# Scores of the first attention in four 32-row tiles: half-heads in blocks of partitions instead of masked keys

## Chip, core and metric

One Trainium2 chip (trn2), one of its cores. The metric is device time in microseconds of the whole launch. Each figure is the median of several runs; one further execution is profiled.

## What is computed

Four batch rows of 512 tokens with 128 features pass through four blocks, each followed by a residual addition and a layer norm: a differential attention, a feed-forward net with weights and activations quantised to 4 bits, a causal attention with rotary positions (16 query heads, 4 key heads), and a mixture of 8 experts. The change touches the first attention alone:

```python
q, k, v = to_heads(q), to_heads(k), to_heads(v)       # 16 heads of 8
q1, q2 = jnp.split(q, 2, axis=-1)                      # half-heads of 4
k1, k2 = jnp.split(k, 2, axis=-1)
a1 = softmax(einsum('bhsd,bhtd->bhst', q1, k1) * scale)
a2 = softmax(einsum('bhsd,bhtd->bhst', q2, k2) * scale)
out = einsum('bhst,bhtd->bhsd', a1 - lam * a2, v)      # then RMS norm, output projection
```

So there are 32 half-heads, each with 512 x 512 scores over a contraction of only 4 numbers. The scores are computed in bf16, with each number split in three bf16 parts and six products of parts kept (`NTERM = 6`), so a half-head's scores take 6 x 4 = 24 rows of contraction.

## The kernel before

**Rows of the batch.** Each engine runs `body` once for each of the four batch rows (first, a loop of two, last). At the end of a row every engine adds to `row_ended`, SP clears semaphores and opens the next row (`open_row`, L352 its increments). A row holds, in order: the first attention (the loop over `s` from -4 to 17), the end of the previous row's mixture of experts together with this row's first output projection and feed-forward net, and then the second attention, which ends with the projection at L1384. While the second attention runs, the next batch row's first-attention projection is computed, split by POOL into parts (`split_next`) and reordered through DRAM by SP (`store_parts`, `load_terms`).

**Operands of the scores.** 8 groups `g` of 4 half-heads `j`. `qst` and `kst` hold all four half-heads of a group on 96 partitions (6 terms x 16). To pick out one half-head, DVE writes `kpad[:, g, j]`, which is `kst` times a mask that zeroes the 72 rows of the other three (`keys_of_next`, 32 tensor_scalars a row, L546; 24 of them at s == 3 of the second attention and 8 at s == 4). Every scores matmul contracts over all 128 partitions.

**Two passes.** For each half-head and tile of 128 queries, PE first computes scores (L1185, 128 matmuls a row), of which DVE takes the negated maximum along the keys (L726, `mx`). Group by group POOL splits the 128 x 16 maxima into three bf16 parts (`max_parts`), PE transposes them (L1192), DVE copies them out as `mrow` (L732), and SP moves them by DMA into rows 96 to 107 of `qst` (L358). The second pass (L1177, 128 matmuls) computes the transposed scores, with the maxima subtracted by those extra rows; ACT takes the exponential (L981). The values product (L1210) follows: for each quarter-tile four matmuls write to four blocks of 32 output partitions; ACT copies the result out (L972), PE transposes it (L1199), DVE keeps it (L737).

**The order around it.** PE's instructions are in one hand-written order. At each step (s, c), c from 0 to 3: two scores matmuls of the second pass (banks 0 to 2 in rotation, each waiting for the exponential three before), two of the first pass, 13 steps ahead (banks 3 to 5 in rotation, each waiting for the maximum three before), and in steps c = 1 and 2 one values product of four matmuls. Group g's second pass starts at s = 2g, c = 0 and waits there for its maxima to have landed (`max0_in`); its transposition L1192 and copy L732 stand at s = 2g - 1, c = 1. So one group takes two s, that is eight steps: 16 matmuls and 16 maxima of the first pass, 16 matmuls and 16 exponentials of the second, four values products. The first-pass maxima end at s = 12.

**Row data and SP.** In a row SP issues one DMA at each of the eight groups and waits for it. In the second attention it issues two for each of its four groups (L366); after the second group it issues 2 stores (L323) and 12 loads (L331) for the next row. POOL clears the unused rows 96 to 127 of `kst` and `qst` with three memsets after the third group (`clear_terms`, L451 to L454), while DVE, in rows 1 to 3, runs the scaling of the mixture's layer norm (L640) at s == 1.

## Time and profile before

| | |
|---|---|
| median of 3 runs | 1578.21 us (1576.48 to 1590.58) |
| the profiled execution | 1577.19 us, its span 1575.4 us |
| PE busy | 1289.6 us, 82% of the span |
| DVE busy | 851.7 us, 54% |
| ACT busy | 666.1 us, 42% |
| POOL busy | 107.2 us, 7% |
| mean granted TensorE clock | 0.891 |
| first attention, rows 0 to 3, about | 60 to 180, 396 to 518, 764 to 886, 1134 to 1256 us |

The span is the time from the first to the last instruction; 1.8 us of the profiled execution lie outside it. Busy shares are means over stages with different limits; the stages have to be read one by one.

### The profile page before, as it was taken

The page shows a single profiled execution, that of the slowest core. Times are in us where ns is not written, and L with a number is a line of the kernel's source. Part 1 is how long each engine was busy: PE and PEld are TensorE (multiplying, and loading weights), DVE is VectorE, ACT ScalarE, POOL GpSimd, SP SyncE. Part 2 cuts the span into 40 slices and gives each one's busy share as a digit, 9 for nine tenths or more (in the row PEclk, how much of TensorE's full clock was granted, in tenths as well). Part 3 has the DMA queues.
Part 4 walks back from the last instruction along what each step waited for, and adds up shares of the span by engine and source line. Part 5 has one row for each costly group of instructions (what it writes and reads, how often), then busy time and mean ns, then how long its engine had stood idle before and what let it go on. Part 6 is the DMA issues. An engine that isn't in the chain of part 4 may idle for free.

```text
span 1575.4 us, 19401 instructions
## 1 busy us (share of the span) xinstructions
PE 1289.6 (82%) x7257; PEld 643.8 (41%) x7257; DVE 851.7 (54%) x1816; ACT 666.1 (42%) x1407; POOL 107.2 (7%) x250
## 2 busy tenths in 40 slices
PE   2499458788898998788799899878789899878888
PEld 1122133445122564344322365444422267344556
DVE  6587446333785467433677365624578456633222
ACT  1067323352376442343166542254157643235232
POOL 4000001020000000020000000003000000000000
PEclk6599769799799999889699999889989999879989
DMA  7400000030000000030000000030000000000000
GB/s 149 111 2 2 8 0 1 21 41 2 1 2 2 1 7 1 1 61 9 2 2 2 1 7 1 1 61 2 7 1 2 1 1 1 1 1 1 8 1 8
DMA packets 31731, 21.04 MB, mean 13 GB/s; under 512 B 12873, under 2 KB 29329, under 8 KB 31633
## 3 DMA queue, kind: packets, MB, share of 16 engines
q1 hardware_dynamic: 31632, 19.75, 6.3%
q8 instruction: 59, 0.97, 0.3%
q14 instruction: 40, 0.32, 0.1%
HBM read 14.96 MB, written 4.19 MB: 12 GB/s over the span
## 4 chain that ended last, share of the span: by engine, by line
PE 64%; DVE 18%; ACT 7%; SPq 4%; issue 3%; DMA 2%; POOL 0%; DVEq 0%; POOLq 0%; PEldq 0%; ACTq 0%; another core or an unknown queue 0%
PE ps L1210 8%; PE ps L1142 8%; PE ps L1152 7%; DVE mx L726 6%; PE ps L1177 6%; PE ps L1291 6%; PE ps L1312 5%; PE ps L1185 5%; PE ps L1281 4%; ACT ps L1038 3%; PE ps L1324 3%; DVE mx L843 2%; DVE SH L817 2%; PE ps L1384 2%; ACT PROB L981 2%
## 5 line engine op out<-in xcount | busy, mean ns | idle before, releaser
L981 ACT ACTIVATE PROB<-ps 128x512 f32<-128x512 f32 x512 | 272.4, 606 | 284.0 <-PE ps L1177 283.9
L726 DVE TENSOR_REDUCE mx<-ps 128x1 f32<-128x512 f32 x512 | 318.7, 683 | 86.0 <-PE ps L1185 85.9
L1185 PE MATMUL ps<-KPAD,SH 128*128 128x512 bf16 x512 | 193.8, 431 | 54.9 <-SPq L352 35.0
L1038 ACT ACTIVATE ps<-ps,mx 128x128 f32<-128x128 f32 (+3 forms) x256 | 127.1, 497 | 252.6 <-DVE mx L843 252.6
L1312 PE MATMUL ps<-KPAD,SH 64*128 64x384 f32 (+3 forms) x512 | 171.4, 530 | 58.4 <-ACT ps L1038 50.2
L843 DVE TENSOR_REDUCE mx<-ps 128x1 f32<-128x128 f32 (+3 forms) x256 | 113.6, 486 | 189.8 <-PE ps L1315 189.8
L1177 PE MATMUL ps<-SH,KPAD 128*128 128x512 bf16 x512 | 163.3, 395 | 15.2 <-ACT PROB L981 9.9
L1291 PE MATMUL ps<-SH,KPAD 64*128 64x256 f32 (+3 forms) x512 | 139.5, 536 | 40.1 <-DMA m1row<-mrow 22.9
L1210 PE MATMUL ps<-PROB,v 128*32 128x512 f32 x1024 | 138.0, 614 | 6.8 <-ACT SH L972 4.7
L959 ACT ACTIVATE KPAD<-ps,b_sb 128x512 f32<-128x512 f32 x128 | 87.9, 687 | 126.8 <-PE ps L1142 126.4
L1312 PEld LDWEIGHTS ps<-KPAD,SH 64*128 64x128 f32 x512 | 79.9, 219 | 117.7 <-ACT ps L1038 98.2
L1142 PE MATMUL ps<-xnT,w_sb 128*128 128x512 f32 x256 | 126.9, 632 | 0.4
L1152 PEld LDWEIGHTS ps<-w_sb,KPAD 128*128 128x128 f32 x1024 | 118.7, 192 | 13.4 <-issue 13.4
L1185 PEld LDWEIGHTS ps<-KPAD,SH 128*128 128x128 bf16 x512 | 51.5, 101 | 166.2 <-DVE mx L726 91.6
L1152 PE MATMUL ps<-w_sb,KPAD 128*128 128x128 f32 x1024 | 118.9, 275 | 0.0
L1177 PEld LDWEIGHTS ps<-SH,KPAD 128*128 128x128 bf16 x512 | 40.6, 99 | 168.2 <-ACT PROB L981 143.7
L1056 ACT ACTIVATE PROB<-ps 128x1024 f32<-128x1024 f32 x80 | 81.2, 1020 | 44.4 <-PE ps L1296 44.4
L1324 PE MATMUL ps<-PROB,KPAD 128*64 128x256 f32 (+3 forms) x512 | 77.4, 444 | 12.2 <-DVE SH L832 12.2
L817 DVE SCALAR_TENSOR_TENSOR SH<-ps,bqk,rope_sb 128x512 f32<-128x512 f32 x96 | 67.5, 745 | 34.1 <-PE ps L1281 33.7
L1291 PEld LDWEIGHTS ps<-SH,KPAD 64*128 64x128 f32 x512 | 63.9, 214 | 48.9 <-DMA m1row<-mrow 25.6
L697 DVE SCALAR_TENSOR_TENSOR KPAD<-ps,rt,KPAD 128x128 f32<-128x128 f32 x112 | 31.5, 344 | 72.7 <-PE ps L1152 72.0
L1142 PEld LDWEIGHTS ps<-xnT,w_sb 128*128 128x128 f32 x256 | 43.2, 198 | 66.3 <-ACT KPAD L959 47.1
(175 smaller groups left out, 1361.9 us busy)
## 6 DMA issues: line engine op xcount, KB each, us to landing
SH<-qk_parts SPq DMA_DIRECT2D x48, 128.0 KB, 6.4
qk_parts<-SH SPq DMA_DIRECT2D x8, 384.0 KB, 2.9
w_sb<-in_L_ffn_W_dram SPq DMA_DIRECT2D x1, 2048.0 KB
XN<-in_L_attn_x_dram SPq DMA_DIRECT2D x4, 256.0 KB, 2.9
out_dram<-XP SPq DMA_DIRECT2D x4, 256.0 KB, 2.3
wq_sb<-in_L_attn_Wq_dram SPq DMA_DIRECT2D x1, 512.0 KB, 5.4
rope_sb<-in_rope_dram SPq DMA_DIRECT2D x1, 512.0 KB
wo_sb<-in_L_attn_Wo_dram SPq DMA_DIRECT2D x1, 512.0 KB
```

Source lines behind the costliest of these rows:

```text
L726: dve.tensor_reduce(mx[:, ga % 2, r % 16:r % 16 + 1], ps[:, 3 + r % 3, :], AX, ALU.max, negate=True).then_inc(max0_done, 1)
L843: dve.tensor_reduce(mx[:, ga % 2, col:col + 1], ps[:, A1_BANK[r % 3], 0:w], AX, ALU.max, negate=True).then_inc(max1_done, 1)
L981: act.activation(prob0[:, n % 2, c, k], ps[:, q % 3, :], ACT.Exp, scale=float(HD0) ** -0.5).then_inc(exp0_done, 1)
L1038: act.activation(tile, tile, ACT.Exp, bias=mx[:, (s + 1) % 2, col:col + 1], accum_out=lsum[:, (s + 1) % 2, 0, col:col + 1]).then_inc(sum1_ ...
L1142: pe.matmul(ps[:, f % 2, :], w1_sb[:, e, P * f:P * (f + 1)], xnT[:, :], start=True, stop=True).then_inc(up_ready, 1)
L1152: ins = pe.matmul(ps[:, 2 + d % 2, P * t:P * (t + 1)], hE[:, d % 2, f, P * t:P * (t + 1)], w2_sb[:, d, f, :], start=(f == 0), stop=(f == 3))
L1177: pe.matmul(ps[:, q % 3, :], kpad[:, g, c, P * kt:P * (kt + 1)], qst[:, g, :], start=True, stop=True).then_inc(s0_ready, 1)
L1185: pe.matmul(ps[:, 3 + r % 3, :], qst[:, a // 8, P * qt:P * (qt + 1)], kpad[:, a // 8, j, :], start=True, stop=True).then_inc(a0_ready, 1)
L1210: ins = pe.matmul(ps[32 * j:32 * j + 32, 6, :], v0[:, kt, 2 * (m // 2) + j // 2, :], prob0[:, m % 2, j, c - 1, :], start=(kt == 0), stop=( ...
L1291: pe.matmul(dst[i], k1[half(i), g, lo:lo + P], qT[half(i), 2 * g + pair, lo:], start=True, stop=False)
L1312: pe.matmul(dst[-1], qT[half(r % 2), 2 * g + pair, P * qt:P * (qt + 1)], k1[half(r % 2), g, 0:w], start=True, stop=False)
L1324: ins = pe.matmul(ps[64 * h:64 * h + 64, 6, P * kt:T], v1[:, kt, D1 * s:D1 * (s + 1)], prob1[:, s % 2, 2 * p_ + h, POFF[kt]:POFF[kt] + WID ...
```

## The change

Each half-head of a group gets a block of 32 partitions of its own: block j holds in its rows 0 to 23 the 24 rows of half-head j, and in rows 24 to 26 the three parts of its maxima (`kst` has ones there). A scores matmul contracts over the 27 (second pass) or 24 (first pass) partitions of its block alone. The masked keys `kpad`, their 32 DVE instructions a row and the mask are gone; `clear_terms` is gone, and one memset at the start writes the ones of `kst`. `qst` and `kst` are tensors of their own. Consecutive matmuls go to different blocks (j = q % 4, j = r % 4), and which half-heads form a group has changed, so the maxima's columns, the values' index and the views of the output change with it. The terms are laid out in DRAM by the stores: 12 stores of 128 KB (one for each term of q and k) in place of 2 of 384 KB, and 8 loads of 192 KB in place of 12 of 128 KB. The maxima of a group go to `qst` by three DMAs (one for each part, to four partitions 32 apart), waited for together, instead of one.

```diff
-M_ROW = NTERM * 16
+M_ROW = NTERM * 4
...
-        KPAD = sb("KPAD", [P, NG * HF * T], BF16)
+        KPAD = sb("KPAD", [P, 12288], BF16)
...
-        qst = SH[:, 0:2048].bitcast(BF16).rearrange("p (g n) -> p g n", g=NG)
-        kst = SH[:, 2048:4096].bitcast(BF16).rearrange("p (g n) -> p g n", g=NG)
+        qst = sb("qst", [P, NG, T], BF16)
+        kst = sb("kst", [P, NG, T], BF16)
...
-                for c in range(2):
+                for c, part in enumerate((Q_PART, K_PART)):
                     sp.wait_ge(parts_ready, c + 1)
-                    sp.dma_start(parts_dram[c].rearrange("s p n -> p s n"), split[:, c]).then_inc(parts_out, 16)
-                sp.wait_ge(parts_out, 32)
+                    for t in range(NTERM):
+                        dst = terms_dram[c, t].rearrange("d j g n -> (j g) d n")
+                        sp.dma_start(dst, split[:, c, part[t]]).then_inc(parts_out, 16)
+                sp.wait_ge(parts_out, 16 * 2 * NTERM)
...
-                for c, (dst, part) in enumerate(((kst, K_PART), (qst, Q_PART))):
-                    for t in range(NTERM):
-                        src = parts_dram[1 - c, part[t]].rearrange("(g r) n -> r g n", g=NG)
-                        sp.dma_start(dst[16 * t:16 * t + 16], src).then_inc(terms_in, 16)
+                for c, dst in ((1, kst), (0, qst)):
+                    for j in range(HF):
+                        src = terms_dram[c].rearrange("t d j g n -> j (t d) g n")[j]
+                        sp.dma_start(dst[32 * j:32 * j + M_ROW], src).then_inc(terms_in, 16)
...
                 for g in range(NG):
                     sp.wait_ge(mrow_ready, g + 1)
-                    sp.dma_start(qst[M_ROW:M_ROW + 12, g, :], mrow[:, :]).then_inc(max0_in, 16)
-                    sp.wait_ge(max0_in, 16 * (g + 1))
+                    for s in range(3):
+                        sp.dma_start(qst[M_ROW + s::32, g, :], mrow[16 * s:16 * s + 16, :]).then_inc(max0_in, 16)
+                    sp.wait_ge(max0_in, 48 * (g + 1))
...
             pool.memset(ones3[:, :], 0.0).then_inc(setup_pool, 1)
+            pool.memset(kst[:, :, :], 1.0).then_inc(setup_pool, 1)
...
-                    if not last and g == 2:
-                        pool.wait_ge(mparts_ready, NG + 3)
-                        clear_terms()
...
-                for g in groups:
-                    for j in range(HF):
-                        dve.tensor_scalar(kpad[:, g, j, :], kst[:, g], jmask[:, j:j + 1], None, ALU.mult).then_inc(keys_ready, 1)
...
+                                col = 4 * (r % 4) + r % 16 // 4
...
-                                dve.tensor_reduce(mx[:, ga % 2, r % 16:r % 16 + 1], ps[:, 3 + r % 3, :], AX, ALU.max,
+                                dve.tensor_reduce(mx[:, ga % 2, col:col + 1], ps[:, 3 + r % 3, :], AX, ALU.max,
...
-                    if not last and s in KEYS_AFTER:
-                        keys_of_next(KEYS_AFTER[s])
...
-                                pe.matmul(ps[:, q % 3, :], kpad[:, g, c, P * kt:P * (kt + 1)], qst[:, g, :],
+                                pe.matmul(ps[:, q % 3, :], kst[rows, g, P * kt:P * (kt + 1)], qst[rows, g, :],
...
-                                pe.matmul(ps[:, 3 + r % 3, :], qst[:, a // 8, P * qt:P * (qt + 1)], kpad[:, a // 8, j, :],
+                                pe.matmul(ps[:, 3 + r % 3, :], qst[rows, a // 8, P * qt:P * (qt + 1)], kst[rows, a // 8, :],
...
-                                ins = pe.matmul(ps[32 * j:32 * j + 32, 6, :], v0[:, kt, 2 * (m // 2) + j // 2, :],
+                                ins = pe.matmul(ps[32 * j:32 * j + 32, 6, :], v0[:, kt, 4 * j + m // 4, :],
```

## Rows read from the trace of the kernel before

**Rows 1.** Stretches of the timeline: us, PE (x) PEld DVE ACT POOL busy, PEclk, DMA, GB/s.

```profile
396.00:409.00 13.00, 11.84 (x21) 2.19 (x21) 12.96 (x27) 0.00 (x0) 0.83 (x4) 0.55 0.00 0
...
447.00:459.70 12.70, 12.43 (x70) 3.76 (x70) 10.42 (x20) 9.00 (x18) 0.83 (x4) 1.00 0.01 3
```

**Rows 2.** The chain that ended last, row 1's first attention: start, us on it, what.

```profile
447.52 0.17 PE ps L1192
447.69 0.99 PE ps L1210 x8
448.69 0.54 PE ps L1177 x2
...
460.08 0.17 PE ps L1192
```

**Rows 3.** Timeline of the same period, DVE: start, us, line, operation, operands.

```profile
445.19 3.68 DVE L726 TENSOR_REDUCE mx<-ps 128x1 f32<-128x512 f32 x6 [0.68 <-PE ps L1185]
...
448.79 0.21 DVE L732 COPY mrow<-ps 48x128 bf16<-48x128 bf16 x1
```

**Rows 4.** Timeline, the hop of one DMA from maxima to second pass, row 1.

```profile
408.56 0.85 SPq L358 DMA_DIRECT2D SH<-mrow  x1
...
410.62 1.03 PE L1177 MATMUL ps<-SH,KPAD 128*128 128x512 bf16 x2 [0.82 <-DMA SH<-mrow]
```

**Rows 5.** Timeline, a hop of two DMAs in row 0's second attention.

```profile
308.77 1.45 SPq L366 DMA_DIRECT2D m1row<-mrow  x2
...
311.47 1.72 PE L1291 MATMUL ps<-SH,KPAD 64*128 64x512 f32 x4 [3.04 <-DMA m1row<-mrow]
```

**Rows 6.** Timeline of PE, a pair in two 64-row tiles and its successor.

```profile
644.06 0.64 PE L1296 MATMUL ps<-m1row,ones 64*128 64x512 bf16 x2
644.49 0.64 PE L1312 MATMUL ps<-KPAD,SH 64*128 64x128 f32 x4
```

**Rows 7.** A stretch of row 1's second attention, columns as in rows 1.

```profile
608.00:612.00 4.00, 2.37 (x18) 1.51 (x19) 2.85 (x8) 0.87 (x5) 0.00 (x0) 1.00 0.00 0
```

**Rows 8.** Timeline, the transpositions of groups 1 and 7 in row 1.

```profile
420.95 0.24 PE L1192 MATMUL ps<-identb,mparts 128*48 128x128 bf16 x1
...
498.17 0.24 PE L1192 MATMUL ps<-identb,mparts 128*48 128x128 bf16 x1
```

**Rows 9.** The chain at the ends of row 0 and row 3.

```profile
368.07 2.33 PE ps L1324 x16
371.03 6.38 DVE KPAD L546 x24
...
384.57 7.43 PE ps L1384 x64
...
1470.80 2.30 PE ps L1324 x16
...
1485.57 7.43 PE ps L1384 x64
```

**Rows 10.** The chain up to group 2's hop in rows 1 and 3, second attention.

```profile
687.39 2.33 PE ps L1324 x16
690.82 4.14 DVE XP L640 x3
695.77 1.91 DMA m1row<-mrow
...
1431.93 2.31 PE ps L1324 x16
1438.35 1.89 DMA m1row<-mrow
```

**Rows 11.** Timeline of SP's queue, second attention of row 0.

```profile
315.14 5.53 SPq L331 DMA_DIRECT2D SH<-qk_parts  x12
334.87 27.94 SPq L366 DMA_DIRECT2D m1row<-mrow  x4
```

**Rows 12.** Timeline of SP's queue at the start of the program.

```profile
22.40 5.53 SPq L331 DMA_DIRECT2D SH<-qk_parts  x12
```

More of the change, by code:

```diff
@@ L335, in give_out @@
                 sp.dma_start(out_rows[bass.ds(row, 1)].rearrange("a p t e -> (a p) t e"), XP[:, :, :]).then_inc(row_out, 16)
-            late = [terms_in, kst_edge, keys_ready, mparts_ready, mrow_ready, max1_in, s1_ready, exp1_done, av1_done,
+            late = [terms_in, mparts_ready, mrow_ready, max1_in, s1_ready, exp1_done, av1_done,
                     oT_ready, y_ready, ln_done, row_out, dve_order, pool_order]
@@ L377, in body @@
                 if not last:
-                    sp.wait_ge(terms_in, 16 * 2 * NTERM)
+                    sp.wait_ge(terms_in, 16 * 2 * HF)
                 open_row()
@@ L412, in _ @@
             pool.memset(ones3[:, :], 0.0).then_inc(setup_pool, 1)
+            pool.memset(kst[:, :, :], 1.0).then_inc(setup_pool, 1)
             pool.memset(eps[:, 0:1], LN_EPS).then_inc(setup_pool, 1)
             pool.memset(eps[:, 1:2], RMS_EPS).then_inc(setup_pool, 1)
-            pool.wait_ge(setup_pool, 6)
+            pool.wait_ge(setup_pool, 7)
             pool.memset(v0[:, :, :, HD0:HD0 + 1], 1.0).then_inc(setup_pool, 1)
             for half in range(2):
-                pool.wait_ge(setup_pool, 7 + half)
+                pool.wait_ge(setup_pool, 8 + half)
                 pool.memset(ones3[64 * half:64 * half + 3, :], 1.0).then_inc(setup_pool, 1)
-            pool.wait_ge(setup_pool, 9)
+            pool.wait_ge(setup_pool, 10)
             def next_row(done, n):
@@ L445, in split_next @@
                     pool.tensor_tensor(split[:, c, 2], rem[:, c], split[:, c, 1], ALU.subtract).then_inc(parts_ready, 1)
-            def clear_terms():
-                pool.wait_ge(parts_ready, 2)
-                pool.wait_ge(parts_out, 32)
-                step(pool.memset(kst[96:128], 0.0))
-                settle()
-                pool.memset(kst[M_ROW:M_ROW + 12], 1.0).then_inc(kst_edge, 1)
-                step(pool.memset(qst[96:128], 0.0))
-                settle()
-                pool.wait_ge(kst_edge, 1)
             def body(first, last):
@@ L496, in body @@
                         split_next((1,))
-                    if not last and g == 2:
-                        pool.wait_ge(mparts_ready, NG + 3)
-                        clear_terms()
                 next_row(mparts_ready, NG + NKV)
             split_next((0, 1))
-            clear_terms()
-            next_row(kst_edge, 1)
+            next_row(parts_ready, 2)
             body(True, False)
@@ L614, in _ @@
             setup(dve.tensor_scalar(bqk[:, 1], bqk[:, 1], rot_sign, None, ALU.mult))
-            keys_of_next(range(NG))
             settle_setup()
@@ L758, in body @@
                     experts_input()
-                step(dve.tensor_scalar(rs[:, :, 1::2], rs[:, :, 1::2], lam[:, 0:1], None, ALU.mult)); settle()
+                rs_u = SH2[:, 1152:1280].rearrange("p (a u x) -> p u a x", a=4, u=2)
+                o_u = SH2[:, 0:1152].rearrange("p (a u x d) -> p u a x d", a=4, u=2, d=HD0 + 1)
+                step(dve.tensor_scalar(rs_u[:, 1], rs_u[:, 1], lam[:, 0:1], None, ALU.mult)); settle()
                 for u in range(2):
-                    w = rs[:, :, u::2].rearrange("p g (h a) -> p g h a", a=1).broadcast_to([P, NG * NT, 2, HD0])
-                    step(dve.tensor_tensor(od[:, u], oall[:, :, u::2, 0:HD0], w, ALU.mult))
+                    w = rs_u[:, u].rearrange("p a (x b) -> p a x b", b=1).broadcast_to([P, 4, 4 * NT, HD0])
+                    step(dve.tensor_tensor(od[:, u], o_u[:, u, :, :, 0:HD0], w, ALU.mult))
                 settle()
@@ L889, in body @@
                         step(dve.tensor_tensor(X[:, :, :], X[:, :, :], bow, ALU.add))
-                    if not last and s in KEYS_AFTER:
-                        keys_of_next(KEYS_AFTER[s])
                 dve.wait_ge(oT_ready, 2 * NKV)
                 settle()
-                if last:
-                    next_row(oT_ready, 2 * NKV)
-                else:
-                    next_row(keys_ready, HF * NG)
-            next_row(keys_ready, HF * NG)
+                next_row(oT_ready, 2 * NKV)
+            next_row(v0_ready, 1)
             body(True, False)
@@ L980, in body @@
                             act.wait_ge(s0_ready, q + 1)
-                            act.activation(prob0[:, n % 2, c, k], ps[:, q % 3, :], ACT.Exp,
+                            act.activation(prob0[:, n % 2, q % 4, q % 8 // 4], ps[:, q % 3, :], ACT.Exp,
                                            scale=float(HD0) ** -0.5).then_inc(exp0_done, 1)
```

46 lines of the change are left out of this document (21 added, 25 removed).

## Prediction

> **What bounds the kernel now.** I read the page first, for the busy shares. PE leads with 82%, but the shares are means over unlike stages, so I next asked for the busy times of the first attention alone. In its steady part PE is busy 12.43 of 12.70 us, DVE 10.42, ACT 9.00, at the full clock (1.00, that is 2.4 GHz) [rows 1]. The chain that ended last shows the same: it stays on PE from one transposition L1192 to the next, 460.08 - 447.52 = 12.56 us for one group of four half-heads [rows 2]. In that period lie four values products of 0.99 us (4.0), transpositions (0.6 with those of the output) and sixteen pairs of scores matmuls, which take the other 7.8: 0.49 a pair, one right after a values product 0.54 [rows 2]. 512 columns at 2.4 GHz are 0.213 us, so the matmuls of a pair run one after the other. So PE is the bound here, and its scores are more than half of it.
>
> What comes next if they get cheaper is DVE: six maxima back to back take 3.68 us, 0.613 each [rows 3], so sixteen of them and the copies cannot go under 10.4 [rows 1]. The most that the change can give in this loop is therefore about 2.1 us a period, six periods a row, four rows: 50 us of 1575. The lead-in before it is on DVE already: 12.96 of 13.00 us [rows 1], and gains nothing.
>
> **The scores matmuls.** Two matmuls in different 64-row tiles already run at once in this kernel: a bf16 pair over 512 columns starts at 644.06 and its successor at 644.49, 0.43 us later, at the half clock, where 512 columns of a single one are 0.427 [rows 6]. Four tiles of 32 rows are not in the trace. I bound a step's four matmuls (now two pairs, 0.97 us) by 0.22 (all at once) and 0.97 (none), and take 0.3, since each step's four lie in four different blocks and banks but wait for different engines. The Trainium skill (TensorE: Matmul & The Clock Gate, Part 3) gives 3.07 times for four row tiles; by it the estimate is 0.28, which would change nothing below. PE's work in a period then falls from 12.4 to 4.0 + 8 x 0.3 + 0.6 = 7.0 us, and PE waits instead of working.
>
> **The hop of the maxima.** Each group's second pass waits for the maxima to go round: DVE copy, SP, DMA, PE. One DMA takes 2.06 us from SP's issue to the matmul (410.62 - 408.56) [rows 4]. Two cost 2.70 (311.47 - 308.77), since an issue holds SP for 0.72 [rows 5]. The change makes three. Their issue price is not in the trace; they have fewer pieces each, so I bound it by 0.46, the price of the large loads [rows 11], and by 0.85, the single one here [rows 4]. That gives 2 x 0.50 + 1.96 = 2.9 to 2 x 0.85 + 1.96 = 3.7 us; I take 3.4, from the pair, which is the nearest row.
>
> This hop was hidden in PE's order and now it is not. After DVE's copy of group g+1 (0.2 us, estimated from the like copies) PE has only two steps left before it stands at the second pass of g+1. Behind that wait in PE's order stand the first pass's matmuls, so DVE runs dry as well: it has four maxima left (2.45 us) against 3.4. From PE's release to the next copy DVE must then take twelve maxima. So the period has a chain of its own: 0.2 + 3.4 + 0.5 (first matmul to DVE) + 12 x 0.613 = 11.5 us. This, and not DVE's 10.4, is the new floor, 1.1 under the 12.56. ACT (9.0) stays below.
>
> **The clock.** PE will be busy 7.0 of 11.5 us and stand still for about 1.8 us in one piece at the hop (3.4 less the two steps). Now it is busy nearly all the time at 1.00 [rows 1]. The rows pull both ways: 2.37 busy of 4.00 us goes with 1.00 in the second attention [rows 7], while the lead-in, PE busy 11.84 of 13.00 with single matmuls paced by DVE, has 0.55, the half clock [rows 1]. I expect one fall to the half clock (1.2 GHz) in most periods. What it costs: the values product of 0.99 us becomes 2.0, once or twice, of which DVE's three banks (1.84 us of maxima) hide the larger part. I take 0.8 us a period, with 0 and 2 as bounds. Period: 12.3.
>
> **The first attention, summed.** In row 1 the stretch from group 1's transposition to group 7's is 498.17 - 420.95 = 77.2 us [rows 8], six periods of 12.56 and 1.8 us of extras (a norm on DVE, a slow first period). With 12.3 it is 73.8, and the norm, now on the chain, leaves about 0.4: 74.2, so 3 us saved, in each of rows 1 to 3. In row 0 there are no extras and the longer hop shows once at group 0 (1.4): 1 us. At group 0 of the other rows DVE's wait grows likewise, but there ACT's table loads hold PE later anyway. After the maxima end, pairs of second-pass scores and values products alternate with ACT; 0.8 us less a row, 3 in all. Sum: 9 + 1 + 3 = 13 us. Bounds: a period of 11.3 (short hop, full clock) gives 24 more; 14 gives 41 less.
>
> **The masked keys.** 24 of DVE's 32 instructions lie at s == 3 and take 6.38 us, 0.27 each [rows 9]. They are on the chain: the copy of the next values product waits behind them, and PE behind that. Row 3 prepares no next row and is what remains without them: from the same values product to L1384 it takes 1485.57 - 1470.80 = 14.77 us, row 0 takes 384.57 - 368.07 = 16.50 [rows 9]. So 6.4 us of work is worth 1.7, three times: 5 us. The other eight lie beside the 7.43 us of L1384 and are free either way.
>
> **The memsets of POOL.** In rows 1 and 2 DVE's scaling of the norm, four short instructions, runs beside `clear_terms` and three of them hold the chain for 4.14 us; it stands ahead of the copy that feeds the next hop [rows 10]. The way from the values product to the hop is 695.77 - 687.39 = 8.38 us there and 1438.35 - 1431.93 = 6.42 in row 3, which has no memsets [rows 10]. So 2.0 us twice: 4. Where the memsets stay without a norm (row 0), nothing.
>
> **The transfers.** In a row 12 stores replace 2 and 8 loads 12: six more issues of 0.46 us [rows 11] and twice the stored bytes, behind the second hop. SP's next duty comes at 334.87, and the old loads end at 320.7 [rows 11], so 14 us of cover; even 8 us more of waiting and issuing stays inside. Were it gone, the third hop would be late by the difference. At the start of the program there is no cover: SP's queue is the chain there until the first row opens, and the old loads begin at 22.40 [rows 12]. Ten more stores add 4.6 us, four fewer loads give 1.8 back, and the doubled bytes land later, 1 or 2 us: 4 us lost, bounds 2.8 and 8. The new 128-partition memset of POOL there lies before anything that it delays.
>
> **Sum.** 13 + 5 + 4 - 4 = 18 us off the profiled execution's 1577.2 (span 1575.4 and 1.8 around it): 1559. The median before, 1578.2, is 1 us above that execution.
>
> **Rivals.** (a) The clock holds, or the three issues are cheap. For it: rows 7, where PE is busy 59% at 1.00. Against: the standstill at the hop is longer than any in the loop now. Period 11.3 to 11.7, so 24 periods shorter by 0.8 in the middle: 1559 - 19 = 1540, far end 1535. Chance 0.22. (b) The clock is at half for a large share of the loop. The Trainium skill (TensorE: Matmul & The Clock Gate, Part 1) says that throttled is the default and that activity releases it; here that would mean that relieving PE slows it. As a mechanism of this kernel: the values products then cost 2.0 each and the scores 0.5 a step, 8 + 4 + 1.2 = 13.2 us of PE work, and with the standstill of 1.8 the period is 15.0 if always cold and about 13.4 if half the time. At 13.4 the loop loses 1.1 x 24 = 26 against my 12.3: 1585, inside 1%. It decides against the change from a period of about 13.7 on (1593), and always cold gives 1559 + 65 = 1624. For it: the lead-in's 0.55. Against: a cold PE is busy nearly all of its time, and in this trace it came back to 1.00 when it was. Chance of slower by over 1%: 0.15. (c) The 32-row matmuls do not overlap, so that the change doesn't do what it says: then a period is PE's 12.4 and the standstill, about 13.9, or 1597. Against: the pair of rows 6. Chance 0.05. (d) Hop and clock together just eat the gain, period 12.8 to 13.5: 1571 to 1588. Chance 0.18. My forecast, a period of 12.0 to 12.8: 1552 to 1571, has 0.40.
>
> **How the numbers follow.** 1% is 16 us, about what a measurement of this kernel tells from no change. Faster by over 1% is under 1562: all of (a) and some 0.35 of the forecast's cases: 0.57. Within 1%: the rest of the forecast, (d), and a little of (c): 0.25. Slower: 0.18. The range reaches from near (a)'s far end, 1537, to 1592, which leaves (b)'s cold cases and part of (c) outside. The likeliest case's own range is 1552 to 1571.
>
> **What would show it.** In the profile after: transpositions L1192 12.3 us apart (now 12.56), PE busy about 60% in the loop, SP's three issues and the matmul 3.4 us after the first, DVE idle about 1 us in a group with the DMA as releaser; a granted clock in the loop that alternates; the first maximum of row 0 some 4 us later than 60; a second attention that ends like row 3's in every row. The prediction is wrong if the period is near 10.4 (the hop is covered), or over 13 (the clock), or if the start of the program costs more than 8 us.

## The result, and the profile after

| | before | after |
|---|---|---|
| median of 20 runs each | 1581.78 us (1575.84 to 1590.58) | 1590.17 us (1583.35 to 1601.45) |
| the profiled execution | 1577.19 us, span 1575.4 | 1594.19 us, span 1592.4 |
| PE busy | 1289.6 us, 82% | 1281.6 us, 80% |
| DVE busy | 851.7 us, 54% | 805.3 us, 51% |
| mean granted TensorE clock | 0.891 | 0.826 |

The ratio of the two is 1.0049, 95% interval 1.0029 to 1.0069: half a per cent slower, where 1.1% faster was forecast. Medians here and below are over all runs, while ratios leave out those more than 1.5% above the fastest of the same kernel. The two profiled executions differ by twice the difference of the medians, 17 us. In the changed kernel the second pass is L1153 (was L1177), the first pass L1162 (L1185), the maxima L703 (L726), the transposition of the maxima L1169 (L1192), the values product L1187 (L1210), the hop's DMAs L357 (L358), and the first matmul of the mixture of experts, which follows the attention in rows 1 to 3, L1116 (L1142); in row 0 the output projection follows, L1204 (L1227).

From the page of the changed kernel: busy time of each engine, the granted clock in 40 slices, and the groups of the attention's matmuls (busy us, mean ns | idle before, what ended most of it).

```profile
PE 1281.6 (80%) x7257; PEld 618.5 (39%) x7257; DVE 805.3 (51%) x1688; ACT 664.8 (42%) x1407; POOL 68.0 (4%) x239
PEclk6578769799587899799678599889868699879989
...
L1162 PE MATMUL ps<-kst,qst 24*128 24x512 bf16 x512 | 177.7, 483 | 56.3 <-SPq L350 37.9
...
L1187 PE MATMUL ps<-PROB,v 128*32 128x512 f32 x1024 | 192.4, 837 | 7.4 <-ACT SH L946 4.1
L1153 PE MATMUL ps<-qst,kst 27*128 27x512 bf16 x512 | 155.4, 466 | 46.5 <-ACT PROB L955 30.3
```

The same from the page of the kernel before:

```profile
PEclk6599769799799999889699999889989999879989
...
L1210 PE MATMUL ps<-PROB,v 128*32 128x512 f32 x1024 | 138.0, 614 | 6.8 <-ACT SH L972 4.7
```

A matmul of the values product, whose shape and number the change leaves alone, takes 837 ns on the mean instead of 614, 54 us more busy time in all. The clock slices say why: where the first attentions lie, most slices of 7 to 9 come down by one to four tenths.

Stretches of the third batch row (called row 2, the first being row 0): first from the transposition of group 0 to that of group 7 (the loop), then from there to about the end of the attention (the tail). Columns as in [rows 1]. Kernel before, then after:

```profile
775.00:866.00 91.00, 85.05 (x438) 25.10 (x437) 70.32 (x126) 60.40 (x114) 5.79 (x28) 0.94 0.01 2
866.00:891.00 25.00, 18.85 (x115) 6.58 (x115) 7.67 (x31) 15.20 (x29) 0.00 (x0) 0.95 0.01 1
```

```profile
784.00:875.00 91.00, 77.52 (x440) 17.91 (x439) 71.33 (x127) 60.52 (x115) 5.80 (x28) 0.76 0.01 2
875.00:908.00 33.00, 26.92 (x113) 7.84 (x112) 7.24 (x30) 14.68 (x28) 0.00 (x0) 0.55 0.00 1
```

The loop is as long as before, with 7.5 us less work on PE but a clock of 0.76. The tail has the same order of instructions and takes 8.9 us longer (33.51 against 24.62), at 0.55. Its chain after, in row 2 (start, us on it, what), shows PE's own matmuls with ACT between them; each values product has 1.9 us on it, against 0.99 in [rows 2]:

```profile
886.21 1.86 PE ps L1187 x8
888.07 0.54 PE ps L1153 x2
888.61 1.87 PE ps L1187 x8
890.48 0.58 PE ps L1153 x3
...
891.54 0.82 ACT PROB L955 x2
...
903.09 0.59 ACT SH L946
```

The whole difference of the profiled executions, summed over the four rows from the first instructions of each line (the second attention is taken up to the first matmul of its output projection):

| stretch | before | after | change | forecast |
|---|---|---|---|---|
| start of the program to the first maximum | 60.1 | 63.2 | +3.1 | +4 |
| loop, groups 0 to 7 | 359.0 | 356.5 | -2.4 | -10 |
| tail, group 7 to the first matmul after the attention | 102.0 | 127.5 | +25.5 | -3 |
| from there to the end of the second attention | 880.8 | 871.7 | -9.1 | -9 |

These make +17.1, against 17.0 between the spans; what the table leaves out is 173.5 us in both. The tails are 28.13, 24.62, 24.62 and 24.62 us before and 30.44, 30.06, 33.51 and 33.51 after.

### The profile page after: what moved, and what is told of

Its sections match the earlier page's. It is cut to its first block, busy times and chain, and to the rows that moved or that the text cites. A ratio compares the mean times of both kernels' runs of the same rounds, so it can differ in the third digit from the quotient of the medians.

```text
span 1592.4 us, 19325 instructions
## 1 busy us (share of the span) xinstructions
PE 1281.6 (80%) x7257; PEld 618.5 (39%) x7257; DVE 805.3 (51%) x1688; ACT 664.8 (42%) x1407; POOL 68.0 (4%) x239
## 4 chain that ended last, share of the span: by engine, by line
PE 62%; DVE 17%; ACT 9%; SPq 5%; issue 4%; DMA 3%; POOL 0%; DVEq 0%; POOLq 0%; PEldq 0%; ACTq 0%; another core or an unknown queue 0%
PE ps L1187 11%; PE ps L1116 8%; PE ps L1126 7%; PE ps L1268 7%; DVE mx L703 6%; PE ps L1289 5%; PE ps L1153 5%; PE ps L1258 4%; PE ps L1301 4%; ACT PROB L955 3%; ACT ps L1012 3%; DVE mx L822 2%; DVE SH L796 2%; PE ps L1361 2%; SPq L392 2%
## 5 line engine op out<-in xcount | busy, mean ns | idle before, releaser
L703 DVE TENSOR_REDUCE mx<-ps 128x1 f32<-128x512 f32 x512 | 318.6, 683 | 102.9 <-PE ps L1162 101.3
L1162 PE MATMUL ps<-kst,qst 24*128 24x512 bf16 x512 | 177.7, 483 | 56.3 <-SPq L350 37.9
L1289 PE MATMUL ps<-KPAD,SH 64*128 64x512 f32 (+3 forms) x512 | 173.6, 537 | 58.7 <-ACT ps L1012 50.5
L1187 PE MATMUL ps<-PROB,v 128*32 128x512 f32 x1024 | 192.4, 837 | 7.4 <-ACT SH L946 4.1
L1153 PE MATMUL ps<-qst,kst 27*128 27x512 bf16 x512 | 155.4, 466 | 46.5 <-ACT PROB L955 30.3
L1153 PEld LDWEIGHTS ps<-qst,kst 27*128 27x128 bf16 x512 | 33.2, 94 | 261.6 <-ACT PROB L955 200.4
L1116 PE MATMUL ps<-xnT,w_sb 128*128 128x512 f32 x256 | 127.4, 634 | 0.4
L1162 PEld LDWEIGHTS ps<-kst,qst 24*128 24x128 bf16 x512 | 37.9, 94 | 120.5 <-DVE mx L703 73.6
L796 DVE SCALAR_TENSOR_TENSOR SH<-ps,bqk,rope_sb 128x512 f32<-128x512 f32 x96 | 67.5, 745 | 31.7 <-PE ps L1258 31.4
L1116 PEld LDWEIGHTS ps<-xnT,w_sb 128*128 128x128 f32 x256 | 43.4, 199 | 66.7 <-ACT KPAD L933 47.2
```

Of the source, the lines that this page charges most:

```text
L703: dve.tensor_reduce(mx[:, ga % 2, col:col + 1], ps[:, 3 + r % 3, :], AX, ALU.max, negate=True).then_inc(max0_done, 1)
L1116: pe.matmul(ps[:, f % 2, :], w1_sb[:, e, P * f:P * (f + 1)], xnT[:, :], start=True, stop=True).then_inc(up_ready, 1)
L1153: pe.matmul(ps[:, q % 3, :], kst[rows, g, P * kt:P * (kt + 1)], qst[rows, g, :], start=True, stop=True).then_inc(s0_ready, 1)
L1162: pe.matmul(ps[:, 3 + r % 3, :], qst[rows, a // 8, P * qt:P * (qt + 1)], kst[rows, a // 8, :], start=True, stop=True).then_inc(a0_ready, 1)
L1187: ins = pe.matmul(ps[32 * j:32 * j + 32, 6, :], v0[:, kt, 4 * j + m // 4, :], prob0[:, m % 2, j, c - 1, :], start=(kt == 0), stop=(kt == 3))
L1289: pe.matmul(dst[-1], qT[half(r % 2), 2 * g + pair, P * qt:P * (qt + 1)], k1[half(r % 2), g, 0:w], start=True, stop=False)
```

## The experiments

Times are medians, ratios those to the kernel before in the same series, with their 95% intervals. The median of the kernel before lies between 1578.77 and 1583.98 us in these series, so kernels of different series are better compared by their ratios. Of each edit the main lines are shown. "Tail" and "loop" are the stretches above; where four numbers stand, they are rows 0 to 3.

**Fill the tail.** The changed kernel with one matmul over the full array added to each step of the tail, into a bank that nobody reads.

```diff
+                        if 13 <= s <= 16:
+                            if s == 13 and c == 0:
+                                pe.wait_ge(max0_done, 16 * NG)
+                            pe.matmul(ps[:, 3, :], kst[:, 0, 0:P], kst[:, 1, :], start=True, stop=True)
```

> The changed kernel, with one more matmul (128 partitions, 512 columns, into the unused bank 3, read by nobody) in each of the 16 steps of s = 13 to 16, after the first attention's maxima have ended. Theory (clock): the loss sits after group 7's transposition, where PE, relieved of half of its scores time, stays at the half clock (0.55 and 0.69 there in the changed kernel, 0.95 before) and the values products cost 1.93 us in place of 1.00. The added work should bring the clock back: the stretch from group 7's transposition to L1116 falls from 33.5 and 30.0 us to about 25 in rows 1 to 3, and the total by 15 to 22 us to 1568 to 1575, faster than the kernel before. Rival (tiling drains or ACT bound the tail): 16 more matmuls of 0.21 to 0.43 us only add work; the stretch stays at 30 to 35 us and the total is 1590 to 1600.

1588.02 us (10 runs), 1.0042 (1.0007 to 1.0076). Tails 29.02, 28.02, 29.92, 29.93 at a clock of 0.89, 0.87, 0.77, 0.77. So added work over all rows of the array raises the clock of the tail and shortens it by 1.4 to 3.6 us, less than the 5 to 8.5 forecast. The total gains nothing that can be told.

**All four matmuls of a step in one block.** PE gets its old amount of work back, since the tiles no longer overlap, but with 24 and 27 rows.

```diff
-                                j, kt = q % 4, 2 * (n % 2) + q % 8 // 4
+                                j, kt = c, 2 * (n % 2) + k
...
-                                j, qt = r % 4, r % 16 // 4
+                                j, qt = (a + 3) % 4, 2 * (a % 8 // 4) + u
```

> The changed kernel with only the order of half-heads changed: the four scores matmuls of a step lie in the same block of 32 partitions (j = c for the second pass, the same block for the first pass), so they can't overlap. Contraction stays 27 and 24 rows, keys and transfers stay as changed. Clock theory: PE is busy with scores as long as before (0.85 us a step), so the clock comes back to about 0.9 in the first attention and the tail to about 25 us; the loop's period is PE's 12.5 to 13. Total 1565 to 1578, faster than the changed kernel by 12 us or more although its matmuls no longer overlap. Rival 1 (the clock follows the rows in use, 27 of 128): it stays at half for much of the loop, and serial matmuls at half clock give 1610 or more. Rival 2 (the clock is not the cause): without overlap the period rises, total 1595 to 1610.

1816.07 us (4 runs), 1.147 (1.138 to 1.157): 15% slower, with periods of 21.02 us. A stretch of one period in row 1, columns as in [rows 1]:

```profile
541.00:562.00 21.00, 21.00 (x73) 4.48 (x69) 10.46 (x18) 9.06 (x17) 0.81 (x5) 0.50 0.00 1
```

and three successive lines of PE's timeline there:

```profile
526.83 1.03 PE L1153 MATMUL ps<-qst,kst 27*128 27x512 bf16 x2
527.66 1.05 PE L1162 MATMUL ps<-kst,qst 24*128 24x512 bf16 x2
528.64 1.94 PE L1187 MATMUL ps<-PROB,v 128*32 128x512 f32 x8
```

PE is busy in all of the 21.00 us, its scores run one after the other (0.83 us from one pair to the next), and the clock stays at 0.50. I had expected that a busy PE brings the clock back. Here it doesn't: of the 21 us some 13 (sixteen pairs of 0.83) go to matmuls over 24 and 27 rows. The standstill at the hop is not what holds the clock here: there is none.

**The hop alone.** The kernel before, its one DMA of the maxima split in three.

```diff
-                    sp.dma_start(qst[M_ROW:M_ROW + 12, g, :], mrow[:, :]).then_inc(max0_in, 16)
-                    sp.wait_ge(max0_in, 16 * (g + 1))
+                    for s in range(3):
+                        sp.dma_start(qst[M_ROW + 4 * s:M_ROW + 4 * s + 4, g, :], mrow[16 * s:16 * s + 16, :]).then_inc(max0_in, 16)
+                    sp.wait_ge(max0_in, 48 * (g + 1))
```

> The kernel before, with its one DMA for the maxima of a group split into three of 4 partitions each, waited for together, as in the changed kernel: the longer hop alone. The hop should take 2.9 us instead of 2.06 (the changed kernel's issues take 0.52 us each). In PE's full order the slack is about 0.8 us, so if the hop is only a small part of the loss the total is within 5 us of the kernel before (1582 +- 5). Rival (the hop is the loss): the period rises by about 0.9 us, six times four, and the total is 1595 or more.

1594.12 us (10 runs), 1.0084 (1.0043 to 1.0126). Each period grows by 0.2 us, 12.56 to 12.75. In its profile, whose span is 23.6 us longer than that of the kernel before, the loops are 7.8 us longer in all and the tails 2.2; the rest lies outside the first attention. The three DMAs take 0.63 us each to issue here (median; 1.96 to 2.13 for the three). The total lies between the two expectations. So the longer hop has a price even where PE has other work behind it, and it isn't what lengthens the tail by 25 us.

**Fill the loop too.** As the first, and one full-array matmul ahead of each step's first-pass pair.

```diff
+                                if u == 0 and s >= 0:
+                                    pe.matmul(ps[:, 3 + r % 3, :], kst[:, 0, 0:P], kst[:, 1, :], start=True, stop=True)
```

> As the first run, and in addition one matmul of 128 partitions and 512 columns in each step with first-pass scores from s = 0 on, written to the bank of that step's first matmul just ahead of it (which overwrites it). It leaves PE's real work as changed and adds about 1.7 us of it in a period. Clock theory: the clock in the loop rises from 0.74 to 0.88 to nearly 1.00, the period falls from 12.0 to 13.9 to about 11.5 to 12.0, and the total is 1555 to 1568. Rival: the hop's standstill still throws the clock to half, and the added work only costs: no better than the run with the tail filled, 1570 to 1580.

1802.88 us (4 runs, 1802.21 to 2223.92), 1.139 (1.127 to 1.151). The periods are 21.35 us at 0.50. A full-array matmul between the two narrow pairs of a step ends the overlap of the pairs with each other: each of the step's three pieces now follows the one before by 0.54 us, as these lines of PE's timeline show. (The two matmuls of a pair still overlap; in one block a pair took 0.83.) One such matmul a step doesn't bring the clock back in the loop, and the total is far from the forecast 1555 to 1568.

```profile
528.04 0.60 PE L1153 MATMUL ps<-qst,kst 27*128 27x512 bf16 x2
528.58 0.61 PE L1167 MATMUL ps<-kst 128*128 128x512 bf16 x1
529.12 0.60 PE L1168 MATMUL ps<-kst,qst 24*128 24x512 bf16 x2
```

By these lines about 12 of the 21.35 us go to matmuls over 128 rows (eight added ones of 0.54 and four values products of 1.9, an estimate), and the clock is 0.50 all the same.

**The rows alone undone.** The changed kernel, all of its scores contracted over 128 partitions again.

```diff
-                                rows = slice(32 * j, 32 * j + M_ROW + 3)
+                                rows = slice(0, P)
...
-                                rows = slice(32 * j, 32 * j + M_ROW)
+                                rows = slice(0, P)
```

> The changed kernel with one thing undone in the scores matmuls: all of them contract over all 128 partitions instead of 24 or 27. (It leaves out the separation of the half-heads: each scores tile is the sum over the four of its group, and the exponential's scale is 1e-9 so that all stays finite; instructions, sizes, waits and transfers are otherwise the changed kernel's.) The run with all four of a step in one block showed PE fully busy at 0.5 through the loop, so a busy PE alone does not hold the clock. Theory (the clock follows how much of the array the matmuls drive): with full rows the clock in the loop is 0.94 to 0.96 as before, the period about 12.75 as in the kernel before with the three-part hop, the stretch after group 7 about 25 us, and the total 1575 to 1590. Rival (the cold clock comes from something else in the change, the operands' place, their ones, the three-part hop): the clock stays at half and the total is over 1750, as in the one-block run, since the matmuls cannot overlap.

1571.58 us (10 runs), 0.9969 (0.9932 to 1.0005). The same two stretches of row 2:

```profile
777.00:868.00 91.00, 84.36 (x437) 24.67 (x436) 70.29 (x126) 60.16 (x114) 5.83 (x28) 0.94 0.01 2
868.00:894.00 26.00, 19.65 (x115) 6.10 (x114) 7.34 (x30) 15.34 (x30) 0.00 (x0) 0.92 0.01 1
```

The number, order and columns of the operations are those of the changed kernel. Besides the rows three things differ: the exponential is scaled by 1e-9, so that all probabilities are near 1, `qst` is zeroed once, and the matmuls of a step no longer overlap. Clock 0.94 and 0.92 instead of 0.76 and 0.55, periods 12.55, tails 28.10, 25.85, 25.82, 25.78. The overlap isn't the cause of the low clock, since the run in one block has none, keeps PE without a gap, and is at 0.50; nor are the values, since the kernel before computes the real ones over 128 rows at 0.94. The zeroing stands at the start of the program. What is left is the matmul over 24 or 27 rows in a block of 32. Whether it is the number of rows or the addressing of a 32-row block that counts, no run separates.

**The rows in the tail alone, and in the loop alone.** Two kernels that split the run before at s = 13: in the first the tail is over 128 rows and the loop narrow, in the second the reverse (there the first pass is wide too).

```diff
+                                rows = slice(0, P) if s >= 13 else slice(32 * j, 32 * j + M_ROW + 3)
...
+                                rows = slice(0, P) if s < 13 else slice(32 * j, 32 * j + M_ROW + 3)
...
+                                rows = slice(0, P)
```

> The new kernel with the scores matmuls over all 128 partitions from step s = 13 on (the tail, second pass only); the loop keeps its 24 and 27 rows. As in the run with all rows wide, the separation of the half-heads is left out there, the exponential is scaled by 1e-9 and qst is zeroed at the start; neither changes the number or size of the operations. Theory 1 (the narrow contraction of the tail's own matmuls keeps the clock down in the tail): tails of 25 to 27 us at a clock of 0.85 or more in rows 1 to 3 (now 30.1, 33.5, 33.5 at 0.56 to 0.68), loop as now (0.75 to 0.81, periods near 12.5); total 15 to 22 us under the new kernel, ratio to the kernel before 0.992 to 0.996. Theory 2 (the tail inherits the loop's clock, or stays low because PE waits for ACT there): tails stay at 30 to 33.5 us at 0.56 to 0.7; ratio 1.004 to 1.006.

> The complement: scores matmuls over all 128 partitions up to step s = 12 (both passes), and the 27 rows in four blocks from s = 13 on. The same parts are left out as in the run before. Theory 1: the loop is that of the kernel before (periods 12.55, clock 0.94 or more), and then the clock falls inside the tail, although it came in warm: tails of 29 to 33 us at 0.6 to 0.75; ratio to the kernel before 1.000 to 1.006. Theory 2 (the tail inherits the loop's clock): tails of 24.5 to 26 us at 0.9 or more; ratio 0.994 to 0.998. It also shows whether the values in the scores (here nearly constant probabilities) have a part in the clock: if they did, this tail too would be at 0.9.

Tail wide: 1578.86 us (10 runs), 0.9978 (0.995 to 1.0006), tails 29.69, 25.79, 25.76, 25.76. Loop wide: 1586.9 us (10 runs), 1.0028 (0.9995 to 1.0062), tails 28.91, 28.47, 27.15, 26.95. Loop and tail of row 2 in the first:

```profile
784.00:876.00 92.00, 79.17 (x437) 17.87 (x437) 70.52 (x126) 59.99 (x114) 5.83 (x28) 0.76 0.01 2
876.00:902.00 26.00, 19.49 (x114) 6.24 (x114) 7.66 (x31) 15.08 (x29) 0.00 (x0) 0.91 0.00 1
```

and in the second:

```profile
779.00:871.00 92.00, 83.77 (x430) 24.84 (x438) 70.66 (x126) 60.41 (x114) 5.80 (x28) 0.95 0.01 2
871.00:898.00 27.00, 20.47 (x114) 6.05 (x114) 7.21 (x30) 15.14 (x29) 0.00 (x0) 0.79 0.00 1
```

A tail of wide matmuls comes out at 0.91 although the loop ahead of it ran at 0.76. A tail of narrow ones falls to 0.79 although it came in from a loop at 0.95: its values products take 1.11 us at 878.72 and 1.93 at 880.29. So the tail's own matmuls set most of its clock; the probabilities are near 1 in both runs, so their values don't make this difference. The second run's tails, 26.95 to 28.91 us at 0.78 to 0.83, lie between the ranges of the two theories: what the tail inherits from the loop has a part too. But the two don't simply add. Summed over the rows from group 0 to the end of the attention:

| loop / tail | wide | narrow |
|---|---|---|
| wide | 464.0 | 472.6 |
| narrow | 468.3 | 484.1 |

The narrow tail costs 8.7 us behind a warm loop and 15.8 behind a cool one. One cell is not like the others: narrow with narrow is the changed kernel with its real probabilities, the other three have them near 1. With real ones, wide with wide is 461.0 (the kernel before), and the narrow loop is 356.5 us where it is 361.3 with those near 1, so in these two the values matter little; for a narrow tail behind a narrow loop no run shows it. The first of these two kernels was expected 15 to 22 us under the changed one and came out 11 under it in the median (0.7% by the ratios); its attention stretches alone give 15.8, the low end. The profiled execution of the second is the fastest of its ten (1578.17 us), that of the first the slowest (1586.10), so these sums hold for the stretches, not for the totals.

**The kernel before without `clear_terms`.** `kst` gets its own tensor with ones written once, and the contractions stop at row 96 or 108, so that POOL's memsets can go.

```diff
-                    if not last and g == 2:
-                        pool.wait_ge(mparts_ready, NG + 3)
-                        clear_terms()
...
-                                pe.matmul(ps[:, q % 3, :], kpad[:, g, c, P * kt:P * (kt + 1)], qst[:, g, :],
+                                pe.matmul(ps[:, q % 3, :], kpad[0:M_ROW + 12, g, c, P * kt:P * (kt + 1)], qst[0:M_ROW + 12, g, :],
```

> The kernel before with one part of the change alone: the memsets of POOL in each row (clear_terms) taken away. kst gets a tensor of its own with its ones written once, the first pass contracts over rows 0 to 95 (the maxima's rows left out) and the second over rows 0 to 107, so nothing need be cleared; masked keys and the single DMA stay. Theory: the 2.0 us of DVE behind the memsets, in rows 1 and 2, and nothing else: 3 to 6 us less than the kernel before, 1576 to 1580. If the narrower contraction by itself costs clock, the loop's period and the stretch after group 7 grow even at 96 rows: over 1590.

1579.77 us (10 runs), 1.0024 (0.9977 to 1.0072). The interval between the hops of groups 1 and 2 of the second attention fell from 28.0 to 26.0 us in rows 1 and 2, the predicted 2.0. The total doesn't show these 4 us, which are less than the width of its interval. Contractions over 96 and 108 rows keep the clock (0.887, before 0.891).

**An earlier hop, at a price.** To hide the hop, I moved the first pass one step ahead (`A_LEAD` 14), and the transposition with it.

```diff
-A_LEAD = 13
+A_LEAD = 14
...
-                        if c == 1 and s % 2 == 1 and -1 <= s <= 13:
+                        if c == 0 and s % 2 == 1 and -1 <= s <= 13:
```

> The changed kernel with the hop of the maxima started one step earlier: the first pass runs 14 steps ahead instead of 13, and transposition and copy stand at c = 0 instead of c = 1. If the exposed hop sets the period where the clock is up (DVE waiting on the DMA), a period falls by 0.6 to 1.2 us and the standstill shrinks, 24 periods less one more lead step of 1.2 us a row: 1570 to 1580. If the clock sets it (values products of 1.9 us), the period stays at 12 to 13.9 and the total at 1585 to 1600.

1631.48 us (4 runs), 1.039 (1.028 to 1.051). I had overlooked the parity: with an even lead both pairs of a step lie in the same two blocks, and the first pass starts only behind the second, 0.23 us later at the full clock, where in the changed kernel the two start within 0.01 (444.88 and 444.89 in a timeline shown further down):

```profile
470.95 0.39 PE L1153 MATMUL ps<-qst,kst 27*128 27x512 bf16 x2
471.18 0.38 PE L1162 MATMUL ps<-kst,qst 24*128 24x512 bf16 x2
```

The first period of a row is 10.2 to 10.3 us, the shortest of the others 11.29, and most take 13 to 17.6; the loops' clock is 0.63 to 0.73. With two full-array matmuls a step in its tail it was no better:

> Both at once, and two added matmuls a step instead of one from s = 13 to 16. With one a step the stretch after group 7 fell by 2 to 3.6 us (33.5 to 29.9, 30.1 to 28.0) and its clock rose from 0.56 to 0.77 and from 0.68 to 0.87. Theory: with two the clock there reaches 0.9 or more and the stretch 26 to 28 us, so 5 to 8 us less than the run with the early hop alone. Rival: PE is then full there and the added work itself costs, no better than one a step.

1632.90 us (4 runs), 1.036 (1.028 to 1.045); tails 31.68, 29.38, 29.10, 29.39 at 0.90 to 0.94. The clock came up as forecast, the tails stayed over the 26 to 28 us.

**An earlier hop, by two steps.** The lead is odd again.

```diff
-A_LEAD = 13
+A_LEAD = 15
...
-                        if c == 1 and s % 2 == 1 and -1 <= s <= 13:
-                            g = (s + 1) // 2
+                        if c == 3 and s % 2 == 0 and -2 <= s <= 12:
+                            g = (s + 2) // 2
```

> The earlier hop once more, without the fault of the run before it: with a lead of 14 steps the parity of the first pass flipped, so that both pairs of a step lay in the same two blocks (its first-pass pair starts 0.40 us after the other one instead of with it). Here the first pass runs 15 steps ahead and transposition and copy stand at c = 3 of the step group before (two steps earlier), so the four blocks of a step differ again and the hop has two more steps of cover. Theory: periods of 11.0 to 11.5 us where the clock is up, and 12 to 14 where it is not, since values products at the half clock then set them; two lead steps more (2.5 us a row). Total 1575 to 1590. If the exposed hop had been the main loss, all periods would be 10.5 to 11.3 and the total under 1565.

1578.97 us (10 runs), 0.9957 (0.9922 to 0.9992), inside the forecast total and 11 us under the changed kernel. The ratio is that of seven runs; over all ten the median is 0.9987 of the kernel before's 1581.08. The same with two full-array matmuls a step in the tail:

> The same with two added matmuls (128 partitions, 512 columns, read by nobody) a step from s = 13 to 16, which in the run with the lead of 14 held the clock there at 0.90 to 0.94 and the stretch after group 7 at 29.1 to 31.7 us. Theory: 3 us less a row than the run beside it, so 8 to 12 us less in all, 1565 to 1580. Rival: the added matmuls cost what the clock gives back, within 5 us of the run beside it.

1575.68 us (10 runs), 0.9968 (0.9939 to 0.9997). PE's timeline of this kernel, the transpositions of groups 3 to 5 in row 1:

```profile
449.92 0.24 PE L1174 MATMUL ps<-identb,mparts 128*48 128x128 bf16 x1
...
460.64 0.24 PE L1174 MATMUL ps<-identb,mparts 128*48 128x128 bf16 x1
...
471.35 0.24 PE L1174 MATMUL ps<-identb,mparts 128*48 128x128 bf16 x1
```

Periods of 10.71 us, near DVE's 10.4: PE no longer stands at the hop. But rows 0 and 1 have only two such periods each and rows 2 and 3 one; most of the others, where the clock is at half for a part of them, take 12 to 16 us. These two are the only kernels of the study whose whole interval lies below 1, by 0.03 to 0.8%. With the three longest runs of the first counted (1585 to 1590 us) its gain over the kernel before is no longer clear, so what is shown is that the earlier hop takes back the loss of the change, not that it makes a faster kernel. Whether the fill adds anything to the lead can't be told from these intervals.

## Why the prediction was wrong

**The scores matmuls: right.** The four tiles of a step run at once. Timeline of PE after, row 1:

```profile
444.88 0.39 PE L1153 MATMUL ps<-qst,kst 27*128 27x512 bf16 x2
444.89 0.39 PE L1162 MATMUL ps<-kst,qst 24*128 24x512 bf16 x2
445.21 1.07 PE L1187 MATMUL ps<-PROB,v 128*32 128x512 f32 x8
```

Four matmuls take 0.33 us of PE (445.21 - 444.88), against 0.3 forecast and 0.97 before. Rival (c) is out. By the Trainium skill (TensorE: Matmul & The Clock Gate, Part 3) the estimate was 0.28; the trace agrees roughly, with 0.33.

**The hop: right in kind, 0.5 us too dear.** Timeline after, row 1:

```profile
411.37 1.81 SPq L357 DMA_DIRECT2D qst<-mrow  x3
...
414.30 0.61 PE L1153 MATMUL ps<-qst,kst 27*128 27x512 bf16 x2 [1.70 <-DMA qst<-mrow]
```

414.30 - 411.37 = 2.93 us, at the lower bound of 2.9; an issue costs 0.53 (median; 0.52 to 0.70). PE stands there, and DVE behind it, as forecast. The chain of the period in row 1 shows it: six maxima, copy, SP, DMA, and then values products at half speed.

```profile
446.71 2.39 DVE mx L703 x4
449.10 1.28 DVE mx L703 x2
450.38 0.13 DVE mrow L709
450.57 0.53 SPq L357
451.14 0.53 SPq L357
451.71 1.61 DMA qst<-mrow
...
455.00 1.53 PE ps L1187 x8
...
457.07 1.83 PE ps L1187 x8
```

**The period: its floor right, its mean too low.** 12.3 us was said. The transpositions of row 1 stand 13.05, 13.87, 12.02, 12.63, 13.88, 13.50 and 13.31 us apart, those of row 0 11.19, 13.53, 12.28, 11.03, 12.25, 12.54 and 11.74. The floor of 11.5, or a little less with the shorter hop, shows in row 0 (11.03, 11.19). But the mean of all 28 is 12.73, against 12.82 before. In row 1 the six periods from group 1 to group 7 take 79.2 us, where 74.2 was forecast and the kernel before takes 77.2. PE is busy 77.52 of 91.00 us in row 2's loop, 85% and not the 60% named as a sign, because a cool PE takes longer for the same work. I priced the clock at 0.8 us a period for one fall; 0.75 to 0.81 over whole loops is more, and the loops save 2.4 us where 10 were in the sum (9 + 1). That term fails by 8 us.

**The tail: the step that failed.** The sum had "0.8 us less a row, 3 in all": it counted the cheaper pairs and gave no clock for this stretch, which leaves the values products at 0.99 us. It is 25.5 us more instead, an error of 28.5, and this one term is larger than the whole forecast gain. I had treated the clock only where PE stands still, in the loop. Rival (b) put the clock right in kind, but in the loop too: it said that relieving PE slows it, and gave 1585 for half the time at half the clock. The loop's clock of 0.75 to 0.81 is about what it had, but the loop didn't grow by its 26 us, it shrank by 2.4, and the loss came in the tail, of which (b) says nothing; that its 1585 is near the measured 1590 is luck. And its mechanism, little work, can't be the whole. The kernel in one block has PE at work without a gap and 0.50; the changed kernel with its rows undone is as busy in its loop and at 0.94 to 1.00. The cause is the narrow contraction: with the rows undone in the tail alone, the tails of rows 2 and 3 fall from 33.51 to 25.76 us and their clock rises from 0.56 to 0.91. Rows aren't the whole either: the lead-in of the kernel before is over 128 rows, paced by DVE, and at 0.55 [rows 1]. My argument against (b), "a cold PE is busy nearly all of its time, and in this trace it came back to 1.00 when it was", was drawn from stretches of matmuls over 64 or 128 rows, and the case of 21.00 of 21.00 us at 0.50 refutes it for narrow matmuls. The Trainium skill (TensorE: Matmul & The Clock Gate, Part 1) has activity release the throttle. The runs agree only if a matmul over 24 rows counts for less than one over 128; in the sense of PE's busy share they disagree.

**Keys and memsets: right in kind, the sum in part by luck.** 9 us were forecast for the two together, 9.1 measured over the whole stretch to the end of the second attention; from the hop of group 1 to that end it is 13.0. In the chain of the changed kernel, row 1:

```profile
704.74 2.31 PE ps L1301 x16
...
711.19 1.97 DMA m1row<-mrow
...
743.71 2.31 PE ps L1301 x16
...
758.49 1.60 PE ps L1361 x12
```

711.19 - 704.74 = 6.45 us, where [rows 10] had 8.38 with memsets and 6.42 without; 758.49 - 743.71 = 14.78, where [rows 9] had 16.50 with the keys and 14.77 without. Both reach the value of row 3, as said. Over all rows the stretch from the last hop to the projection, 23.20, 24.53, 23.21 and 21.51 us before, is 21.48 to 21.51 after: 6.5 us from the keys, where 5 was in the sum. The interval between the hops of groups 1 and 2 falls by 1.9 us in each of rows 1 and 2. But row by row the whole stretch changes by -1.1, +0.1, -8.4 and +0.3 us, where -1.7, -3.7, -3.7 and 0 were forecast: the interval between the hops of groups 0 and 1, in which neither lies, is anything from 31.4 to 38.6 us in the kernels here, the kernel before included. That 9.1 is so near 9 says little.

**The start: right, by two errors that cancel.** The first maximum comes 3.1 us later. The timeline of SP's queue after, against the loads' start at 22.40 in [rows 12]:

```profile
18.67 7.68 SPq L321 DMA_DIRECT2D qk_terms<-SH  x12
27.88 1.54 SPq L329 DMA_DIRECT2D kst<-qk_terms  x4
29.46 1.59 SPq L329 DMA_DIRECT2D qst<-qk_terms  x4
```

The stores cost 7.68 / 12 = 0.64 us each, more than the 0.46 assumed, but the eight loads only 0.39, less than it, and the sum came out near.

**What stays open.** How the clock's fall depends on the number of rows between 27 (0.50) and 96 (no change) wasn't tried, nor a matmul over few rows outside a 32-row block. What the clock follows exactly isn't shown: the filled loop is at 0.50 with more than half of its time in matmuls over 128 rows, and four overlapped narrow tiles (0.76) do better than the same tiles one after the other (0.50). Nor can I say why a narrow tail costs twice as much behind a cool loop. The profiled executions differ by 17 us and the medians by 8; a part of the tail's 25 us belongs to that one execution, though the runs with the rows undone in the tail and everywhere, 0.7% (11 us) and 0.8% (13 us) under the changed kernel by the ratios, show that the loss there is real, and about as large as the whole difference of the medians. (The medians themselves would say 11 and 19, but they are from different series.)

## What to carry to other kernels

Price a change of matmul shape in two parts: the time that the tiles save, read at the clock of before, and the price of that clock falling, over every stretch in which the new shape runs, including those in which PE isn't the bound. Price all the other matmuls of the stretch at up to their time at half speed: here the 1024 matmuls of the values products, whose shape nobody touched, cost 54 us of PE more, and PE's busy time as a whole fell by only 8. And when PE stops being the bound, move the next wait (here the hop, by two steps) in the same change; it gave back 11 us.

## What was not expected of the hardware

- The granted clock falls with narrow contractions in 32-row blocks: PE busy 21.00 of 21.00 us with mostly 24- and 27-row matmuls, 0.50; the changed kernel's order over 128 rows, 24.72 busy of 25.00, 1.00 (stretch 440 to 465 of that run); over 96 and 108 rows the mean clock is 0.887, with 128 it is 0.891.
- One full-array matmul between two pairs in 32-row tiles ends the overlap of the pairs: 0.54 us for each piece at the half clock. With the added work and the lower clock the period goes from 12.5 to 21.35 us.
- Pairs of 32-row matmuls overlap only if the pair behind goes to other blocks than the one ahead: with both in the same two the second starts 0.23 us later at the full clock, and the kernel, whose hop had moved by a step as well, took 1631 us against 1590.
